# The first expert's routing weights in the first block: through memory instead of through TensorE

## What is computed

```python
x = x + 0.5 * ffn(layernorm(x))      # blocks 0 to 3
x = x + attention(layernorm(x))      # 16 heads, causal
x = x + 0.5 * ffn(layernorm(x))      # blocks 4 to 7

def ffn(x):                          # 8 experts, every token in every expert
    weights = golden_weights(x)      # (tokens, 8), one routing weight per token and expert
    h = silu(x @ Wg[e]) * (x @ Wu[e])
    return sum_e weights[:, e] * (h @ Wd[e])
```

## Time and profile before

| what | us |
|---|---|
| median of 3 runs (lowest, highest) | 736.88 (736.26, 736.93) |
| the profiled execution, its own time | 736.52 |
| its span, first to last instruction | 734.8 |
| TensorE matmul busy | 728.4 |
| VectorE busy | 468.0 |
| GpSimd busy | 417.5 |
| ScalarE busy | 340.9 |

### The profile page before, as it was taken

The page is one execution under the profiler, slowest core; times in us unless marked ns, Lnnn a source line. Parts: engine busy times, 40 slices in busy tenths (PEclk is TensorE's granted clock), DMA queues, the critical chain, the costliest instruction groups (busy, mean ns, idle before and its releaser), DMA issues.

```text
span 734.8 us, 13763 instructions
## 1 busy us (share of the span) xinstructions
PE 728.4 (99%) x4714; PEld 592.2 (81%) x4714; DVE 468.0 (64%) x1308; ACT 340.9 (46%) x661; POOL 417.5 (57%) x497
## 2 busy tenths in 40 slices
PE   8999999999999999999999999999999999999998
PEld 7888889877788777778778778778777778888887
DVE  6976966866567947686448657955658434563333
ACT  5447346344375543755434557445454433323222
POOL 3678384544764535845546843464564665656663
PEclk9999999999999999999999999999999999999999
DMA  9474234634243644145442333634323333214321
GB/s 290 145 247 144 76 109 132 175 117 145 74 112 116 177 127 122 59 130 147 142 136 88 120 99 115 178 110 145 104 78 95 98 106 114 74 72 136 116 95 58
DMA packets 69878, 90.47 MB, mean 123 GB/s; under 512 B 13232, under 2 KB 49456, under 8 KB 69808
## 3 DMA queue, kind: packets, MB, share of 16 engines
q1 hardware_dynamic: 67472, 89.03, 39.1%
q10 hardware_dynamic: 2336, 0.56, 0.3%
HBM read 72.36 MB, written 17.04 MB: 122 GB/s over the span
## 4 chain that ended last, share of the span: by engine, by line
PE 91%; DVE 5%; issue 1%; ACT 1%; DMA 0%; POOL 0%; DVEq 0%; ACTq 0%
PE ra L828 15%; PE ra L830 15%; PE ra L829 15%; PE dn L860 8%; PE dn L861 8%; PE dn L862 8%; PE ra L970 5%; PE ra L958 5%; PE ra L942 5%; PE ra L789 2%; PE ra L931 1%; PE ra L932 1%; PE ra L933 1%; PE ra L918 1%; PE ra L920 1%
## 5 line engine op out<-in xcount | busy, mean ns | idle before, releaser
L1455 POOL TENSOR_TENSOR hid<-hid,wb 128x512 f32<-128x512 f32 x124 | 161.8, 1307 | 146.5 <-DVE hid L1304 139.4
L1459 POOL TENSOR_TENSOR ht_lo<-hid,ht_hi 128x512 fp32r<-128x512 f32 x124 | 163.0, 1317 | 114.4 <-ACT ht_hi L1070 114.0
L828 PE MATMUL ra<-xt_hi,wgu_hi 128*128 128x512 f32 x508 | 216.2, 426 | 0.3 <-DVE hid_b L1304 0.3
L830 PE MATMUL ra<-xt_lo,wgu_hi 128*128 128x512 f32 x508 | 200.5, 395 | 0.0
L829 PE MATMUL ra<-xt_hi,wgu_lo 128*128 128x512 f32 x508 | 200.4, 395 | 0.0
L1296 DVE SCALAR_TENSOR_TENSOR hid<-hid,ra 128x512 f32<-128x512 f32 x125 | 85.5, 685 | 136.7 <-ACT hid L1062 135.7
L860 PE MATMUL dn<-wd,ht_hi 128*128 128x256 f32 x496 | 149.3, 301 | 0.6 <-POOL ht_lo L1459 0.6
L861 PE MATMUL dn<-wd,ht_hi 128*128 128x256 f32 x496 | 139.2, 281 | 0.0
L862 PE MATMUL dn<-wd,ht_lo 128*128 128x256 f32 x496 | 139.1, 280 | 0.0
L1070 ACT ACTIVATE ht_hi<-hid 128x512 fp32r<-128x512 f32 x124 | 77.8, 629 | 128.5 <-POOL hid L1455 103.5
L1361 DVE CUSTOM_DVE_ANT_0 junk<-ra,mask 128x128 bf16<-128x128 f32 (+3 forms) x256 | 112.5, 484 | 26.7 <-PE ra L942 26.3
(11 more groups left out here) (178 smaller groups left out, 827.8 us busy)
## 6 DMA issues: line engine op xcount, KB each, us to landing
wd<-wd_parts SPq DMA_DIRECT2D x56, 512.0 KB, 3.5
wb<-wts_rows SPq DMA_DIRECT2D x63, 256.0 KB, 3.7
qk_parts<-parts SPq DMA_DIRECT2D x32, 192.0 KB, 2.3
q_st<-qk_parts SPq DMA_DIRECT2D x96, 64.0 KB, 2.3
k_st<-qk_parts SPq DMA_DIRECT2D x96, 64.0 KB, 2.3
wd_parts<-wd SPq DMA_DIRECT2D x8, 512.0 KB, 3.5
ctx_rows<-cx SPq DMA_DIRECT2D x16, 256.0 KB, 2.7
stage<-in_Wg SPq DMA_DIRECT2D x8, 256.0 KB, 4.3
```

Source lines behind the costliest of these rows:

```text
L828: mm(b_, w_hi, xt_hi[q % 2][:, c, :], start=c == 0, stop=False)
L830: last = mm(b_, w_hi, xt_lo[q % 2][:, c, :], start=False, stop=c == KT - 1)
L1455: nc.gpsimd.tensor_tensor(tb, tb, wb[m % NWB][:, :], ALU.mult).then_inc(hw_done, 1)
L1459: nc.gpsimd.tensor_tensor(ht_lo[n % NHT][:, :], hidden(n)[:, :], f32(ht_hi[n % NHT][:, :]), ALU.subtract).then_inc(lo_done, 1)
```

## The change

`NWP` becomes 0. The item *wbp* and its four products and its ScalarE copy are gone; the first expert's `wb` in block 0 is loaded from `wts_rows` like all others. The planner's due time of block 4's preparation (its stats, normalisation, routing) is moved from 1.52 to 1.18.

```diff
-NWP = 1
+NWP = 0
...
-    put(1.60, ("wbp", 0))
...
-        start = CB * (q - 1) + {1: Q1, 2: 3.10, 4: 1.52, 5: 7.85, 6: 6.41, 7: 8.21}.get(q, 5.0)
+        start = CB * (q - 1) + {1: Q1, 2: 3.10, 4: 1.18, 5: 7.85, 6: 6.41, 7: 8.21}.get(q, 5.0)
```

## The result

| what | before | after |
|---|---|---|
| median of 6 runs each (lowest, highest), us | 736.57 (735.80, 737.95) | 740.77 (739.41, 741.68) |
| the profiled execution, its own time, us | 736.52 | 740.95 |
| its span, us | 734.8 | 739.2 |

The changed kernel takes **4.2 us more**: ratio 1.0051, 95% interval 1.0039 to 1.0064. The forecast was +1.8 and 738.7. The sign and the wide range (736.9 to 741.2) held; the size did not, and the forecast's own range, 738.0 to 739.5, was missed. 740.77 lies where the fourth rival stood, at 0.15.

What follows compares the result with a forecast made beforehand. TensorE, never idle, was taken to bound the kernel, so changes in its first 50 us arrive in full: -0.89 - 0.32 + 3.3 + 0.3 - 0.63 = +1.8 us, 738.7; own range 738.0 to 739.5, wide range 736.9 to 741.2.

Steps and rivals of the forecast that it cites:

- the fourth rival: More late than d2: load at 30 or after, VectorE holding GpSimd twice, or swaps adding waits; 739.5 to 741, chance 0.15.
- the saving at 21.4 and at u3: TensorE, chunk 3's up product: 0.89 us of products gone plus 0.32 us idle gone, 1.21 us saved.
- the start of GpSimd: Block 0: first expert's weights come 5.9 us later, so GpSimd starts its first hi at 29.2 instead of 23.27.
- VectorE and GpSimd taking turns: Before chunk 2's down products: VectorE's low part of expert 4's weights holds GpSimd up by 1.15 us.
- d2 starting at 39.10: Chunk 2's down products wait for GpSimd's lo2 from 35.85 to about 39.15: 3.3 us idle.
- The step on d6: Chunk 6's down products no longer wait for GpSimd, saving 0.63 us of idle at 49.83.
- The 0.3 at d3: Chunk 3's down products wait for GpSimd's lo3, ready at 40.8 but wanted at 40.57: 0.25 to 0.3 us idle.
- No other wait before d2: TensorE, 1.21 us early after chunk 3's up product, would reach chunk 2's down products at 35.85 without a wait.
- The clock, given 0.08: Rival: after the pause TensorE falls to 1.2 GHz for 24 matmuls of d2 and d3; +2.8, 741.5 in all, chance 0.08.
- d16, named as the likeliest place and given 0.3: Block 1, chunk 16's down products: likeliest place for an added wait; 0.3 us held possible, left to the range.
- 1.4 us for seven of eight stores: Evidence for a quick store of routing weights: the seven other stores landed in 1.4 us in the median.
- the first rival: Store and load quick, GpSimd starts at 28.2 or sooner, d2 waits 2.3 us or less; 736.9 to 737.7, chance 0.28.

Runs made afterwards that it cites:

- the order at d16: Two halves of gate and up products of chunk 20 moved ahead of chunk 16's down products on TensorE, against the changed kernel: 739.11 us, ratio 1.0034.
- the pause at d2: Three kernels against the changed one: eight idle matmuls behind d1, 739.33 us; u7 ahead of d2, 739.33; first two experts' routing-weight loads ahead of weight loads, 738.31.
- all four together: Changed kernel plus early routing-weight loads, expert 2's low part earlier on VectorE, u7 ahead of d2, two halves ahead of d16: 737.76 us, ratio 1.0008.
- the shifted stream: Changed kernel plus eight 64-column matmuls behind d1 on TensorE, results overwritten, against the kernel with eight of 512 columns: 739.65 us, ratio 1.0040.

## Why the prediction was right and wrong

**Right, and to a tenth or two:** the saving at 21.4 and at u3 (-1.18, forecast -1.21); the store at 22.42; the start of GpSimd (29.31, forecast 29.2, from the landing and the load of the weights as they were measured before); VectorE and GpSimd taking turns, with the low part of expert 4's weights starting at 33.79 (forecast 33.7) and costing GpSimd 1.0 us (forecast 1.15); d2 starting at 39.10 (forecast 39.15). The step on d6 was right as to place, and -0.93 instead of -0.63, because a wait costs more than its idle. The 0.3 at d3 was right for an execution at full clock (0.36 with the due time put back); in the changed kernel's profile the slow clock at d2 covered it.

**Wrong, the terms of the sum:**

- *No other wait before d2.* I followed the chain of the routing weights and did not look at what the four products had covered. VectorE was writing expert 2's low part from 22.78 for 1.22 us in the kernel before, and g4 took it at once when it was ready. TensorE 1.2 us early could only wait there, and did, 0.93. It moved a part of the pause from d2 to g4 (2.29 at d2 where 3.3 were forecast) and so cost nothing itself. The two errors cancel, which was luck, not foresight.
- *The clock, given 0.08.* The fall came in the profiled execution, +1.57 (1.2 beyond the wait at d3 that it covered), and by the clock of the single runs in 4 of the 6, though these 4 are only 0.4 us slower than the other 2 in the median. I set its price, 2.8, from 24 matmuls at half clock; 15 were hit. The argument against it, that full clock was granted in the stretch that held a wait of 0.63 us, says nothing about a pause three times as long. The Trainium skill ("TensorE: Matmul & The Clock Gate", Why this matters for your kernels) asks for short pauses between bursts of matmuls; the runs agree, though the pauses here are shorter than those that the page warns of, and the fall comes behind some of them and not behind others. Over all kernels here whose profile has an idle of 1.58 us or more ahead of a down product in block 0, 23 of 46 runs show a clock of 0.998 or less; of those with new lists and under 1.2 us, 1 of 49. That one had full clock around d2; its clock fell earlier, behind an idle of 1.72 us at 11.08. A run without a trace doesn't say where its clock fell.
- *d16, named as the likeliest place and given 0.3.* It cost 1.55. The cover had shrunk by a half product, 0.7 us, as I wrote, and I had taken the landing of the store as it was, 1.4 us. It became 2.8, since the removed matmuls let a fetch of instructions fall beside it. No row of the kernel before could show that fetch. That landings vary could be seen: the earlier trace rows go from 1.4 to 3.2, and a bound from there would have given 1.5 us for d16.
- *"1.4 us for seven of eight stores".* This reads a median as if it were every value. In the kernel before, too, two of SyncE's seven stores were slow, 3.7 us in block 2 and 3.4 in block 3:

```profile
wts_rows<-wt SPq DMA_DIRECT2D x1, 16.0 KB, 3.7
```

  It is five of eight, and the first rival's 0.28 and the 1.4 taken for block 1 rested on the median.

**The sum by what was measured:** -1.18 + 0.93 + 2.29 + 1.57 - 0.93 + 1.55 = +4.23 in the profiled execution, whose own time is 4.4 above that of the kernel before; the last 0.2 come without a wait behind 672 us. That the medians differ by 4.2 as well is in part chance, since the clock fell in some runs and not in others. The repairs each give back about their share: the order at d16 1.7, the pause at d2 1.4 to 2.4, all four together 3.0. Only the 2.4 and the 3.0 lie clear of the changed kernel's interval.

The first rival fell in the kernel as changed: GpSimd started at 29.31, and no sooner than 29.55 even in the one profile whose store landed in 1.4, because the load goes out behind the weight loads and is slow there. Of the fourth only the added wait in blocks 1 to 4 came, though for another cause than swapped items alone.

**Still open:** what decides in an execution whether the clock falls (due time put back: a pause of 2.68, no fall; the shifted stream: 1.58, a fall); why the store lands 1.0 to 1.1 us behind its last piece where a fetch held this up and 0.4 us behind it otherwise; what delays the stores of blocks 2 and 3; and whether the saving can be had at all, since with all waits of blocks 0 and 1 repaired but four small ones the kernel is only level with the one before.

## What to carry to other kernels

Where one engine is never idle, removing work from it only helps as far as everything it then meets is ready sooner too: look at what the removed work covered, in all engines, before counting it as gain. Here 1.2 us of matmuls were traded for a chain through memory (store 3.0, load to first use 3.8 us), and GpSimd, made to start 6 us later, was late at d2, and at d4 or d18 where d2 or d16 were covered. Price a pause of the matmul engine twice, once for itself and once for the clock behind it. And price a transfer that something waits for with the spread of its landings, not with the median, which hid two slow stores of seven here.

## What the runs showed of the hardware

- The store of block 1's weights, 16 KB, landed in 1.4 us without and in 2.4 to 3.0 with a fetch of instructions (one packet of 16 KB, some 37 in the program) 0.4 to 0.7 us behind its issue: its last two pieces of 512 B started when the fetch was over. Eight matmuls more or fewer on TensorE, 50 us earlier, decided which, and with it whether d16 waited, 1.1 us in the medians. In the midst of other traffic, in blocks 2 and 3, stores of this size took 2.0 to 4.0 us.
- In the kernels with idles of 1.6 to 2.7 us in block 0, 17 of 40 runs show a fall of TensorE's clock to 1.2 GHz. Of their traces two show it behind that idle (2.11 and 1.58 us), for 3.4 us, and four do not (2.03, 2.19, 2.68 and 2.69 us). With an idle of 4.06 us all six runs show it, and the trace has half clock for 6.8 us.
- A wait of TensorE cost 0.2 to 0.3 us more than the idle in its row.
